# Shared-expert chunks in the first pass, routed experts one step earlier, and sums made by accumulating transfers in a fused RWKV and mixture-of-experts layer

## The reference, cut to what matters

```python
xn = layernorm(x)
s  = attention_and_channel_mix(xn)     # two RWKV halves, one after the other along a sequence
g  = silu(shared_expert(xn) + routed_expert(xn))
return x + s * g

# routed_expert: logits = xn @ gate_w.T; top_id = argmax(logits); score = sigmoid(max(logits))
#                the expert top_id (of 8) runs on xn * score, a SwiGLU of width 256
# shared_expert: the same SwiGLU form, one set of weights, on every token
# each RWKV half: layernorm, a shift by one token, mixes, matmuls; the first has a
# recurrence along the 256 tokens (running maximum and two weighted sums)
```

## Time and profile before

| | us |
|---|---|
| median of 3 runs | 583.97 (583.27 to 585.6) |
| the profiled execution | 577.9 |
| its span | 576.1 |
| PE busy | 464.0 (81%) |
| DVE busy | 425.2 (74%) |
| ACT busy | 345.6 (60%) |
| POOL busy | 264.7 (46%) |

### The profile page before, as it was taken

How to read it: one execution, slowest core, us unless ns; L and a number is a source line. 1 busy time by engine, 2 the same in 40 slices (tenths; PEclk the granted TensorE clock), 3 DMA queues, 4 the chain that set the end, 5 groups by cost and what they waited for, 6 DMA issues and landing times. The chain is left out here.

```text
span 576.1 us, 8950 instructions
## 1 busy us (share of the span) xinstructions
PE 464.0 (81%) x2623; PEld 345.9 (60%) x2623; DVE 425.2 (74%) x836; ACT 345.6 (60%) x707; POOL 264.7 (46%) x317
## 2 busy tenths in 40 slices
PE   0989777797979797889898989898989897637661
PEld 0989244564646464787777777777777776425341
DVE  3553795879697977695969596969696968783766
ACT  3776423665646566676776677677777676536441
POOL 6664003657575858461818181818181828210100
PEclk9999988999899999999999999999999999957986
DMA  6329404010000001262727282727272825245482
GB/s 200 110 75 257 96 0 155 22 36 26 33 25 33 31 27 38 62 186 73 221 71 211 84 222 73 209 85 220 73 225 71 226 66 167 73 136 158 128 236 73
DMA packets 68864, 64.97 MB, mean 113 GB/s; under 512 B 5952, under 2 KB 57025, under 8 KB 68816
## 3 DMA queue, kind: packets, MB, share of 16 engines
q1 hardware_dynamic: 63344, 54.31, 34.5%
q0 software_dynamic: 4320, 8.53, 4.2%
q10 hardware_dynamic: 1152, 1.56, 0.8%
HBM read 46.86 MB, written 17.97 MB: 113 GB/s over the span
## 5 line engine op out<-in xcount | busy, mean ns | idle before, releaser
L849 POOL DMA_INDIRECT routed_out<-xh,xs x71 | 91.3, 1286 | 30.2 <-ACT xh L689 16.1
L486 PE MATMUL bank_ring<-xh,ew 128*128 128x128 f32 x568 | 78.6, 281 | 19.9 <-DMA ew<-ex_w 9.3
L486 PEld LDWEIGHTS bank_ring<-xh,ew 128*128 128x128 f32 x568 | 68.8, 191 | 26.9 <-ACT xh L689 15.2
L841 POOL DMA_INDIRECT tokens_by_expert<-xn,pos x64 | 67.2, 1051 | 37.0 <-issue 18.5
L1069 DVE TENSOR_TENSOR kk<-rk 128x512 f32<-128x512 f32 x32 | 26.3, 822 | 54.3 <-ACT rk L650 54.3
L689 ACT ACTIVATE xh<-bank_ring 128x256 f32<-128x256 f32 (+1 forms) x75 | 27.8, 371 | 63.4 <-PE bank_ring L500 62.3
L440 PEld LDWEIGHTS bank_out<-fvw,kk 128*128 128x128 f32 x512 | 60.9, 195 | 8.2 <-issue 8.2
L440 PE MATMUL bank_out<-fvw,kk 128*128 128x128 f32 x512 | 60.8, 278 | 0.0
L823 POOL TENSOR_SCALAR x_sm<-x_mv 128x4 f32<-128x4 f32 x16 | 3.8, 235 | 111.8 <-DVE x_mv L1051 111.8
L470 PE MATMUL bank_ring<-xt,sup 128*128 128x512 f32 x64 | 34.9, 628 | 17.5 <-DVE hs L1085 10.6
L837 POOL TENSOR_TENSOR rw<-den_num,lq 128x512 f32<-128x512 f32 x16 | 20.3, 1269 | 53.8 <-issue 46.5
(11 more groups left out here) (139 smaller groups left out, 1124.0 us busy)
## 6 DMA issues: line engine op xcount, KB each, us to landing
ew<-ex_w SPq DMA_DIRECT2D x71, 384.0 KB, 4.0
xi<-x SPq DMA_DIRECT2D x32, 256.0 KB, 3.7
tokens_by_expert<-pad_row SPq DMA_DIRECT2D x1, 4686.0 KB, 21.2
xs<-tokens_by_expert SPq DMA_DIRECT2D x71, 66.0 KB, 3.6
ew<-routed_out SPq DMA_DIRECT2D x16, 256.0 KB, 3.3
out<-xn SPq DMA_DIRECT2D x16, 256.0 KB, 3.2
routed_out<-xh,xs POOLq DMA_INDIRECT x71, 4.1
tokens_by_expert<-xn,pos POOLq DMA_INDIRECT x64, 2.3
```

The costliest lines, as they stand in the source:

```text
L486: last = nc.tensor.matmul(part(GU[n % 2], q, P), part(w, q, P), xt[:, 0:P], start=True, stop=True)
L841: nc.gpsimd.indirect_dma_start(xs_dram, bass.IndirectOffsetOnAxis(ap=POS[:, t:t + 1], axis=0), XN[:, t * XROW:(t + 1) * XROW], None).then_ ...
L849: nc.gpsimd.indirect_dma_start(routed_dram, bass.IndirectOffsetOnAxis(ap=XS[(n - 2) % NXS][:, CH:CH + 1].bitcast(i32), axis=0), XH[n % NXH ...
```

## The change

What it does, part by part:

- **S pieces.** All 16 shared chunks come before the experts (`EARLY = 16`). Fourteen S (seven chunks) run in the first pass, one in each iteration from c = 2 on; steps 0 to 3 hold four S each, step 4 the last two and the last D. Step 16 has no S any more.
- **Experts** take steps 5 to 13 (`E_STEP = 5`). The 60 scatters that follow step 0 now lie 15 each in steps 1 to 4.
- **x buffers.** `XI` has ten: four of its own and six tiles of the second RWKV half.
- **Routing.** `routing_counts` runs ahead of step 0, `routing_starts` and `routing_rows` early in it. The score is made by exp, ln and exp in place of a sigmoid; the first chunk's second deviation is a power on POOL.
- **Sums by transfers.** The shared output goes from ACT to four staging buffers (the first 512 columns of `EW` 0 to 3) and SP stores it to `ffn_out`. The routed scatter is an indirect transfer on POOL that adds to `ffn_out`; unused rows have places of their own behind it. SP copies x to `out` once, DRAM to DRAM, after shared chunk 8. A final piece Z loads one sum (eight buffers), ACT makes the SiLU, DVE multiplies by s, and POOL issues a transfer of the chunk that adds to `out`.
- **Z pieces**: five in step 14, eight in step 15, none in step 16, four in step 17.
- Weights of expert slots 0, 1, 2 and 4 are loaded ahead; those of slot 3 after the token rows and the last shared store.

```diff
-EARLY, LATE = 14, 16
-E_STEP = 6
+EARLY = 16
+E_STEP = 5
+IN_FIRST = 14
...
+    for c in range(CHUNKS - IN_FIRST, CHUNKS):
+        first[c].append(shared.pop(0))
+    for i in range(E_STEP):
         for k in (0, 2, 4, 6):
-            steps[i][k].append(shared.pop(0))
+            if shared:
+                steps[i][k].append(shared.pop(0))
...
+    for c in range(CHUNKS - 3):
+        steps[CHUNKS - 2 + (c + 3) // 8][(c + 3) % 8].append(("Z", c))
...
             def load_x(c):
-                if c >= 4:
-                    sp.wait_ge(s_xn, c - 3)
-                sp.dma_start(tiles(XI[c % 4][:, :]), rows(x, c)).then_inc(s_xi[c % 4], 16)
+                if c >= NXI:
+                    sp.wait_ge(s_xn, c - NXI + 1)
+                sp.dma_start(tiles(XI[c % NXI][:, :]), rows(x, c)).then_inc(s_xi[c % NXI], 16)
...
+            def store_shared(m):
+                sp.wait_ge(s_sh, m + 1)
+                sp.dma_start(rows(ffn_dram, m), tiles(SO[stage(m)])).then_inc(s_so[stage(m)], 16)
...
+            for m in range(EARLY - 1):
+                store_shared(m)
+                if m == PREFILL:
+                    sp.dma_start(out, x).then_inc(s_pre, 16)
             sp.wait_ge(s_rt, RT_DONE)
-            for n in range(NEW):
+            for n in (0, 1, 2, 4):
+                if n < 4:
+                    sp.wait_ge(s_so[n], 16 * stored(n, EARLY))
                 load_weights(n)
...
+            store_shared(EARLY - 1)
+            sp.wait_ge(s_so[3], 16 * stored(3, EARLY))
+            load_weights(3)
...
             for c in range(CHUNKS):
                 first_transpose(c)
+                if c == CHUNKS - IN_FIRST:
+                    pe.wait_ge(s_wa, 16 * 5)
+                first_shared(c)
                 if c > 0:
                     logits(c - 1)
...
             def final_part(c):
                 if c < CHUNKS:
-                    act.wait_ge(s_fy, c + 1)
-                    nc.scalar.activation(part(XT, c, CHUNK), part(XT, c, CHUNK), ACT.Silu).then_inc(s_fw, 1)
+                    act.wait_ge(s_fin[c % 8], 16 * (c // 8 + 1))
+                    if c >= EARLY:
+                        act.wait_ge(s_fy, c - EARLY + 1)
+                    nc.scalar.activation(FO[c % 8], FO[c % 8], ACT.Silu).then_inc(s_fw, 1)
...
                     nc.gpsimd.indirect_dma_start(
-                        routed_dram, bass.IndirectOffsetOnAxis(ap=XS[(n - 2) % NXS][:, CH:CH + 1].bitcast(i32), axis=0),
+                        ffn_dram, bass.IndirectOffsetOnAxis(ap=XS[(n - 2) % NXS][:, CH:CH + 1].bitcast(i32), axis=0),
                         XH[n % NXH][:, P:P + CH], None,
-                        bounds_check=TOKENS - 1, oob_is_err=False).then_inc(s_yo[n % NXH], 16)
+                        compute_op=ALU.add).then_inc(s_yo[n % NXH], 16)
+
+            def final_part(c):
+                if c > 0:
+                    if c == 1:
+                        pool.wait_ge(s_pre, 16)
+                    pool.wait_ge(s_fv, c)
+                    settle(pool)
+                    nc.gpsimd.dma_start(rows(out, c - 1), xn(c - 1), accum_op=ALU.add).then_inc(s_out[(c - 1) % 4], 16)
...
                 if 0 < i < E_STEP:
-                    scatter(12)
+                    scatter(15)
...
                 if c > 0:
                     dve.wait_ge(s_fw, c)
                     dve.wait_ge(s_s, c)
-                    nc.vector.tensor_tensor(xn(c - 1), tiles(part(XT, c - 1, CHUNK)), xn(c - 1), ALU.mult)\
-                      .then_inc(s_fv, 1)
-                if c < CHUNKS:
-                    dve.wait_ge(s_fr_in[c % 4], 16 * (c // 4 + 1))
-                    dve.wait_ge(s_sh, c + 1)
-                    nc.vector.tensor_tensor(part(XT, c, CHUNK), RR[c % 4], part(XT, c, CHUNK), ALU.add).then_inc(s_fy, 1)
-                if c > 0:
-                    u = (c - 1) % 4
-                    dve.wait_ge(s_fv, c)
-                    dve.wait_ge(s_fx[u], 16 * ((c - 1) // 4 + 1))
-                    nc.vector.tensor_tensor(xn(c - 1), xn(c - 1), tiles(XI[u][:, :]), ALU.add).then_inc(s_fo, 1)
+                    nc.vector.tensor_tensor(xn(c - 1), tiles(FO[(c - 1) % 8]), xn(c - 1), ALU.mult).then_inc(s_fv, 1)
```

More of the change, by code:

```diff
@@ L34 @@
 K_ID, K_TRI, K_ONE, K_E8, K_CAP, K_TILE, K_TOK = 0, 128, 256, 384, 392, 456, 536
[L35 to L38 removed]
+NCST = K_TOK + TILES + NXH
+EARLY = 16
+E_STEP = 5
+IN_FIRST = 14
 def plan():
+    first = [[] for _ in range(CHUNKS)]
     steps = [[[] for _ in range(8)] for _ in range(CHUNKS + 2)]
[L45 to L48 removed]
+    shared = [("S", m, q) for m in range(CHUNKS) for q in range(2)] + [("D", CHUNKS - 1)]
+    for c in range(CHUNKS - IN_FIRST, CHUNKS):
+        first[c].append(shared.pop(0))
+    for i in range(E_STEP):
         for k in (0, 2, 4, 6):
[L50 removed]
+            if shared:
+                steps[i][k].append(shared.pop(0))
     steps[E_STEP][0] += shared
@@ L58, in plan @@
         steps[E_STEP + place // 8][place % 8].append(slot)
-    late = [("S", m, q) for m in range(EARLY, LATE) for q in range(2)] + [("D", LATE - 1, 0)]
-    for k, item in zip((0, 1, 2, 3, 4), late):
-        steps[CHUNKS][k].append(item)
-    for c in range(6):
-        steps[CHUNKS - 1][c + 2].append(("Z", c))
-    for c in range(6, CHUNKS - 3):
-        steps[CHUNKS][c - 6].append(("Z", c))
+    for c in range(CHUNKS - 3):
+        steps[CHUNKS - 2 + (c + 3) // 8][(c + 3) % 8].append(("Z", c))
     for c in range(CHUNKS - 3, CHUNKS + 1):
         steps[CHUNKS + 1][0].append(("Z", c))
-    return steps
-PLAN = plan()
+    return first, steps
+FIRST, PLAN = plan()
 def program(nc, x, vecs, cst, att_w, f_kw, f_vw, gate_w, sh_up, sh_dn, ex_w, out):
@@ L150, in program @@
         HX = [sb(f"hx{u}", EF) for u in range(NHX)]
-        RR = [EW[u][:, 0:CHUNK] for u in range(4)]
+        SO = [EW[u][:, 0:CHUNK] for u in range(4)]
+        FO = SO + [t[:, :] for t in XI[0:4]]
         BK, BV = bank("bank_k"), bank("bank_v")
@@ L169, in program @@
         s_settled = sem("settled")
-        s_xi = [sem(f"x_loaded{u}") for u in range(4)]
+        s_xi = [sem(f"x_loaded{u}") for u in range(NXI)]
         s_bn, s_mv, s_nm, s_ve = sem("x_partial_stats"), sem("x_stats"), sem("x_minus_mean"), sem("x_var_eps")
@@ L255, in sent, with stage, stored @@
             return sum(1 for m in range(2, n) if m % NXH == n % NXH)
+        def stage(m):
+            return (m - EARLY) % 4
+        def stored(u, m):
+            return sum(1 for k in range(m) if stage(k) == u)
         def ring(k):
@@ L502, in expert_slot, with first_shared @@
                     last.then_inc(s_dn, 1)
+            def first_shared(c):
+                for _, m, q in FIRST[c]:
+                    shared_part(m, q)
             def fill(i, k):
@@ L571, in first_xn @@
                     t = c * TPC + j
-                    last = nc.scalar.activation(xn_tile(t), part(XI[c % 4], j, P), ACT.Identity,
+                    last = nc.scalar.activation(xn_tile(t), part(XI[c % NXI], j, P), ACT.Identity,
                                                 bias=NB[:, t:t + 1], scale=RS[:, t:t + 1])
@@ L661, in shared_out @@
                 act.wait_ge(s_sd, m + 1)
-                nc.scalar.activation(part(XT, m, CHUNK), ring(5 * (m + 1) + 2)[:, :], ACT.Copy).then_inc(s_sh, 1)
+                if 4 <= m < EARLY:
+                    act.wait_ge(s_so[stage(m)], 16 * stored(stage(m), m))
+                dst = SO[stage(m)] if m < EARLY else part(XT, m, CHUNK)
+                nc.scalar.activation(dst, ring(5 * (m + 1) + 2)[:, :], ACT.Copy).then_inc(s_sh, 1)
             def shared_part(m, q):
@@ L1096, in final_part @@
             def final_part(c):
+                if EARLY <= c < CHUNKS:
+                    dve.wait_ge(s_fin[c % 8], 16 * (c // 8 + 1))
+                    dve.wait_ge(s_sh, c + 1)
+                    nc.vector.tensor_tensor(FO[c % 8], FO[c % 8], part(XT, c, CHUNK), ALU.add).then_inc(s_fy, 1)
                 if c > 0:
@@ L1178, in _ @@
             first_aggregate(CHUNKS - 1)
+            for c in range(CHUNKS - 3, CHUNKS):
+                first_shared(c)
             time_mixes(0)
```

149 lines of the change are left out of this document (77 added, 72 removed).

## The result

The changed kernel takes 603.88 us (median of 4 runs, 601.14 to 605.3), the kernel before 584.79 us on the same chip: a ratio of 1.034, 95% interval 1.030 to 1.039. It is 3.4% slower. The forecast was 602.7 us. The number came right mostly by chance, as the terms will show: the span was forecast at 594.8 us and is 603.0, and the 7.9 us that I added from the span to the median are 0.9 here: the profiled execution of before was a short one for its kernel (577.9 us), that of after (604.77) lies 0.9 over its median.

The account below looks back on a forecast made before the run. PE bounds the first pass, the chain from `attention_out` to `rw` and `ffn_value` an empty step. 30.7 - 7.6 - 20.0 + 2 + 13.6 = +18.7 on 576.1 gives span 594.8, plus 7.9 makes 602.7 us; range 580 to 620.

Parts of the forecast that it names:

- First pass: Stage up to the last logits: PE is the limit and takes in the moved S and D pieces, +30.7 us.
- iterations of the first pass at less than 5 us: Sign in the first pass: if PE runs its iterations in under 5 us, the forecast is wrong.
- Step 0: Step after the first pass: four of eight DVE products leave, some waits stay; -7.6 us, between -4 and -12.
- Shared steps: Steps 1 to 4 in place of 1 to 5: three more scatters each delay rw, 29.3 us each; -20.0 us.
- Experts: Eight steps with experts: same as before, one step earlier; the adding indirect transfer taken as 0 us.
- The end: Steps 14, 15, 16 and tail: 28.5 + 29.0 + 24.4 + 10.5 = 92.4 us against 78.8 before, +13.6 us.
- A: Rival on final transfers: POOL pays per row, four times 1.05 us each; together +29.8, 632.5 us; chance 0.11.
- B: Rival on steps 14 to 16, tail and shared steps: shortest chains, scatters hidden; sum -3.5, 580.5 us; chance 0.12.
- C: Rival on steps 14 to 16: a step is as long as PE's work; sum -15.5, 568.5 us; chance 0.07.
- PE was not the limit: Sign in the first pass: shown if the last logits, expected near 88 us, end before 80.
- An empty step: Sign for a step without S pieces or experts: if it takes under 24 us, the forecast is wrong.
- start of the experts: First step with experts: slot 3's weights come after row loads and a store; +2 us, between 0 and 4.

Follow-up runs that it names:

- e2: Kernel before with one more 128x512 matmul, its result unread, in each of 14 first-pass iterations: 583.93 us, ratio 1.003.
- e3: Kernel before with ten x buffers, twelve S in the first pass, four in each of steps 1 to 5, none in steps 0 and 16: 583.84 us, ratio 1.005.
- e8: Kernel before with e3's moved S pieces and x buffers plus e7's order of the final pieces: 567.05 us, ratio 0.978.
- e6: Kernel before with 15 scatters in each of steps 1 to 4 and none in step 5: 584.87 us, ratio 1.010.
- e9: The changed kernel run and profiled again, unaltered: 600.02 us, ratio 1.028 to the kernel before.
- e4: Changed kernel with the copy of x to out issued in the first pass, behind the clearing of ffn_out: 596.05 us, ratio 1.027 to the kernel before.
- e1: Changed kernel with plain indirect transfers of the experts' rows in place of adding ones: 585.71 us, ratio 1.012 to the kernel before.
- e10: Changed kernel without the copy of x to out, final transfers writing in place of adding: 597.09 us, ratio 1.024 to the kernel before.
- e5: Kernel before with an added copy of x to a spare tensor, for which the loads of experts' rows wait: 578.92 us, ratio 0.999.
- e7: Kernel before with ACT's SiLU one place behind DVE's sum and DVE's product and last sum one further; no shared piece moved: 566.04 us, ratio 0.976.

## Why the prediction was right, and where it was not

**First pass: right mechanism, term too large (+30.7, measured +18.1).** PE was the limit, but the sum priced 14 iterations at the 2.46 us of the earlier trace rows. That was the slow rate. With the S pieces among them PE comes to the fast one: 2 x 0.86 for an S and some 1.3 to 1.4 for logits and transposes. Of the 49.0 us from 26.6 on, 12 x 1.72 + 6 x 1.79 = 31.4 are shared work; that leaves 17.6 for the logits and transposes, where the sum had 12 x 2.46 + 2.3 = 31.8. The two iterations ahead, at the slow rate, cost 1.5 more than forecast. The forecast had named a sign of being wrong here, iterations of the first pass at less than 5 us, and it came true: those from 26.6 us on take 3.0 us without a down projection and 4.8 with one. The earlier trace rows together gave a hint: eight 128x8 matmuls in 1.71 us beside 0.86 us for two of 128x512 are slow for their size. But no row of before showed the same logits at the other rate, and the column said 1.00. e2 shows it in the kernel before.

**Step 0: right (-7.6, measured -5.1).** It gained less than forecast: PE, busy for 4.5 of 10 us between 80 and 90, was granted 0.53 there, and it waited for DVE. PE's timeline of after in step 0:

```profile
82.62 0.59 PE L374 MATMUL bank_fb<-rt,consts 128*128 128x8 f32 x2 [2.68 <-DVE rt L991]
...
103.05 3.78 PE L454 MATMUL bank_ring<-sdn,hs 128*128 128x128 f32 x16 [6.74 <-DVE hs L1132]
```

A down projection of 1.95 us took 3.78 behind a wait of 6.74 for a product of DVE. Without any S in step 0 (e3, e8) the step is 32.3 us, 5 us shorter.

**Shared steps: half right (-20.0, measured -8.6).** Two of four steps came out at 29.7 and 30.2, near the 29.3 forecast, and e6 gives the scatters' part: 5.6 of the 8.8 us that were put down to them. The four steps are 11.4 us over the forecast, and 10.1 of these are in steps 1 and 3, in waits that the trace gives to no engine. They move about: step 3 is 29.6 in e9 and 29.8 in e4 but 33.6 in e1; step 1 is 34.6 in e9 and 34.4 in e10 but 28.9 in e1 and 30.9 in e4; step 4 is 33.5 in e10. The copy isn't their cause (e5, e10). What is stays open. In the kernel before and the variants of it (e2, e3, e5 to e8) no step from 1 to 4 takes over 29.7 us.

**Experts: the step that failed (0, measured +12.4).** The prediction bounded the adding indirect transfer from "the same instruction on POOL" to twice the landing, looked at one buffer that waits for the landing ("eight `XH` buffers cover even that") and took 0. Both the engine's time and the landing grew. POOL's timeline of after in step 6, the first and last of eight, and `rw`:

```profile
281.88 2.38 POOL L885 DMA_INDIRECT ffn_out<-xh,xs  x1 [0.17 <-issue]
...
297.17 1.55 POOL L885 DMA_INDIRECT ffn_out<-xh,xs  x1 [0.30 <-issue]
299.71 1.27 POOL L869 TENSOR_TENSOR rw<-den_num,lq 128x512 f32<-128x512 f32 x1 [0.99 <-issue]
```

The same place in e1, where the transfers are plain, the last of them and `rw`:

```profile
287.13 0.96 POOL L885 DMA_INDIRECT ffn_out<-xh,xs  x1 [1.71 <-ACT xh L707]
291.23 1.26 POOL L869 TENSOR_TENSOR rw<-den_num,lq 128x512 f32<-128x512 f32 x1 [3.14 <-issue]
```

Undisturbed, one holds POOL for 1.55 us in place of 0.96. Eight of them take POOL from 281.9 to 298.7, 16.8 us against 274.4 to 288.1 = 13.7 in e1. But POOL's row isn't what sets the step. POOL still stands idle for 0.99 us ahead of `rw`, which starts when ACT has made `lq` (298.94 + 0.63 = 299.57):

```profile
298.94 0.63 ACT L637 ACTIVATE lq<-lq 128x512 f32<-128x512 f32 x1
```

`rw` is done at 301.0, and `attention_out` of the next step starts at 304.7, straight behind PE's own work. In each of steps 6 to 12, in after and in e1 alike, `rw` starts 5.0 us ahead of the next `attention_out`.

The time is lost in front of the experts' matmuls (L491), which wait for weights (`ew`). SP issues a load of rows (L309) ahead of the next load of weights, and into a row buffer that an earlier transfer of POOL must have left: it waits for that transfer's landing. SP's issues in step 6, and then PE's last slot of the step:

```profile
284.24 0.34 SPq L315 DMA_DIRECT2D ew<-ex_w  x1
288.48 0.33 SPq L309 DMA_DIRECT2D xs<-tokens_by_expert  x1
289.65 0.34 SPq L315 DMA_DIRECT2D ew<-ex_w  x1
```

```profile
292.71 1.13 PE L491 MATMUL bank_ring<-xh,ew 128*128 128x128 f32 x8 [1.24 <-issue]
```

The load at 288.48 waited 3.9 us, for the landing of the transfer that POOL began at 281.88. By the trace's semaphores that took 6.6 us to land, and 4.6 in e1, where SP waits 1.8 us. The weights issued behind, at 289.65, land at 292.6, and there PE starts the slot, 17.9 us after `attention_out`. In e1 it starts after 16.8 us with next to no wait. That is the 1.0 us between the two steps. Over steps 6 to 12, the waits of SP and PE (in all, times, longest) and the transfers that POOL issued (packets, MB, share of the transfer engines), in after:

```profile
SPq L309 <- DMA ffn_out<-xh,xs: 39.9, 16, 5.2
PE bank_ring L491 <- DMA ew<-ex_w: 13.0, 16, 1.7
PE bank_ring L491 <- issue: 10.9, 7, 1.8
q0 software_dynamic: 8064, 3.67, 18.2%
```

and in e1:

```profile
SPq L309 <- DMA ffn_out<-xh,xs: 14.7, 10, 2.1
PE bank_ring L491 <- DMA ew<-ex_w: 8.8, 13, 1.3
PE bank_ring L491 <- issue: 0.8, 1, 0.8
q0 software_dynamic: 1792, 3.67, 4.7%
```

With its smaller waits for DVE and ACT, PE waits 28.0 us in front of L491 in after and 17.4 in e1: 10.6 more, where the seven steps are 10.3 longer. So e1 shows that the price is the adding, and the traces show where it is paid: in the landing that SP's row load waits for, with the weights queued behind it. The later transfers of a step also start later, since POOL takes longer over each (the fifth of step 6 at 16.3 us after `attention_out`, in e1 at 14.1). No run moves that row load alone, so this link is read and not tested. The other 2.0 of the 12.4 us are in e1 too.

**The end: right mechanism, terms of the right size but one (+13.6, measured +9.3).** The rows of POOL in steps 14, 15 and 17:

```profile
519.69 1.19 POOL L856 TENSOR_SCALAR x_sm<-x_mv 128x4 f32<-128x4 f32 x1
520.86 1.96 POOL L858 TENSOR_TENSOR x_sm<-x_sm,minus_half 128x4 f32<-128x4 f32 x1
...
531.66 3.90 POOL L896 DMA_DIRECT2D out<-xn  x3 [1.16 <-DVE xn L1151]
...
548.05 1.04 POOL L858 TENSOR_TENSOR x_sm<-x_sm,minus_half 128x4 f32<-128x4 f32 x1
...
591.79 5.29 POOL L896 DMA_DIRECT2D out<-xn  x4 [17.53 <-DVE xn L1151]
```

Step 14 is 28.1 us against 28.5 forecast, with the small operations slowed as foretold (1.19 and 1.96). Step 15 is 25.4 against 29.0: there DVE has gaps (busy 18.2 of 25.4 us, in step 14 22.2 of 28.1), the power takes 1.04 again, and most of the 3 us put down to POOL's slowing isn't paid. Step 16 with the tail is 34.7 against 34.9; its parts were off against each other, the landing at 6.9 where 4.4 was put. e7 shows the coupling that the forecast read in the earlier trace rows: once the SiLU doesn't wait in front, step 15 shrinks by 7.4 us, with only the order of the final pieces changed. The change's SiLU needs only a transfer and is free of that wait too; the kernel before can have this gain for itself, without what the adding costs.

**The rivals.** A (POOL pays per row) falls: a transfer of 512 rows holds POOL for 3.90 / 3 = 1.30 us, the value taken, not 4.2. (Its three parts, 11.6, 15 and 3, add up to 29.6, not to 29.8.) The Trainium skill (DMA: Bandwidth & Descriptors, Anatomy of one DMA) says that many descriptors can be issued before their number counts. The trace agrees: 512 rows written cost 0.77 us (3.09 / 4), no more than 128 rows through a list at 0.96. The Trainium skill (SBUF — State Buffer, SBUF: two separate sides) gives 620 ns against 3100 ns for a transfer issued by POOL, alone and beside a copy on DVE. Nothing fivefold shows here: beside a busy DVE the longest of the eight transfers in step 6 takes 2.38 us against 1.55; the tail, where DVE is idle, can't test it. B (chains at their shortest) was near for step 15 (25.4 against 24), but the scatters (e6), the tail and the experts ruled it out. C falls: PE works 12.9 us in a step of 25.4.

**Of what was to show it:** the last logits came at 75.6, under the 80 at which "PE was not the limit". That check was wrong: PE was busy for every microsecond, at another rate. An empty step stayed over 24 us (25.4), and the iterations of the first pass fell under 5 us, as told above. `attention_out` of step 1 came at 113.1 and not near 122, step 5 began at 241.8 (near 240), step 14 at 514.8 and not near 502. The difference of the medians, 19.1 us, is near the sum's 18.7 by luck, twice over. Two misses, 12.6 us too many in the first pass and 12.4 too few in the experts, took each other away. The others (11.4 too few in the shared steps and 2.5 in step 0, against 4.3 too many at the end and 1.5 at the start of the experts) left the span 8.2 us too short, and the 7.9 us that were added for the short profiled execution of before hid that.

## What to carry to other kernels

Before pricing work that is moved in among small matmuls, compare the pitch of a large matmul on both sides, since the rate of PE in the stage may be half that of the stage it comes from, and the new work may raise it. The granted clock of a stretch for which the trace has no record yet says nothing. An instruction that is "the same but adds" has to be priced by its landing too, and that landing followed to everything that waits for it: here it was one queue, in which a row load that waited for it stood in front of the next weights. Where two kinds of work share an engine's fixed order, try moving the waiting piece one place later first: here that alone gave 2.4%, more than all that was moved and merged.
